# Cross-attention and MoE kernel: maxima over partitions by matrix transposes, an earlier load of x for group 1, a new order of small steps in the first group

## The reference

```python
# x, ctx: (4, 1024, 1024) f32; 4096 tokens in all, D = 1024
def fp8_quant_dequant(v):
    scale = 448.0 / max(max(abs(v)), 1e-12)          # one scale for the whole tensor
    return float8_e4m3(clip(v * scale, -448, 448)) / scale

x = x + fp8_qd(layernorm(x)) @ fp8_qd(ctx) + mask    # mask is a bias per batch and column
h = layernorm(x)
x = x + shared_ffn(h) + moe(h)
# shared_ffn: silu(h @ gate) * (h @ up) @ down, inner width 1024
# moe: 32 experts of inner width 512; sigmoid scores plus bias, best 3 of 8 groups, best 4 experts,
#      each expert takes its first 160 tokens (position = running count), silu(G) * U @ W_down, weighted add
```

## Time and profile before

| | us |
|---|---|
| median of 3 runs | 2037.12 (2036.63 to 2037.95) |
| the profiled execution | 2037.94 |
| its span | 2036.3 |
| TensorE busy | 1870.2 (92%) |
| VectorE busy | 1395.4 (69%) |
| ScalarE busy | 896.9 (44%) |
| GpSimd busy | 587.8 (29%) |
| mean granted TensorE clock | 0.991 of full |

### The profile page before, as it was taken

One profiled execution on the slowest core, in us unless ns is written; L12 is line 12 of the kernel. 1 busy time (PEld: TensorE's weight loads), 2 busy tenths in 40 slices (PEclk: granted clock), 3 DMA queues, 4 the chain that ended last, 5 costly groups with the idle time before them and its releaser, 6 DMA issues.

```text
span 2036.3 us, 45113 instructions
## 1 busy us (share of the span) xinstructions
PE 1870.2 (92%) x17857; PEld 1439.3 (71%) x17872; DVE 1395.4 (69%) x2535; ACT 896.9 (44%) x1269; POOL 587.8 (29%) x613
## 2 busy tenths in 40 slices
PE   0038999999999999999999999989999999999997
PEld 0017577678668668767767867858888888888886
DVE  5787775575575576566546535368888888888884
ACT  8564222222222222222212121157777777777774
POOL 2100101210220220220211111136555565655642
PEclk9998999999999999999999999999999999999999
DMA  9925322222222212312211211379999999999993
GB/s 378 373 70 197 95 82 73 84 63 64 84 62 75 93 44 74 94 62 62 76 63 43 63 63 53 135 259 357 371 353 363 368 347 374 349 367 363 355 369 86
DMA packets 93267, 371.94 MB, mean 183 GB/s; under 512 B 21264, under 2 KB 25392, under 8 KB 68560
## 3 DMA queue, kind: packets, MB, share of 16 engines
q1 hardware_dynamic: 68144, 311.16, 39.6%
q0 software_dynamic: 23808, 58.81, 13.2%
q10 hardware_dynamic: 1184, 0.15, 0.0%
HBM read 314.79 MB, written 55.35 MB: 182 GB/s over the span
## 4 chain that ended last, share of the span: by engine, by line
PE 88%; DVE 2%; DMA 1%; issue 1%; SPq 0%; POOL 0%; ACT 0%; POOLq 0%; ACTq 0%
PE ps L1277 52%; PE ps L1288 16%; PE ps L1456 8%; PE ps L1315 5%; PE ps L1464 2%; PE ps L1342 1%; PE ps L1418 1%; PE ps L1360 1%; DMA X<-in_x 1%; DMA BIG<-in_w_up 1%; PE ps L1298 1%; DVE W L966 1%; PE ps L1423 0%; PE ps L1366 0%; POOL out_rows L580 0%
## 5 line engine op out<-in xcount | busy, mean ns | idle before, releaser
L1277 PE MATMUL ps<-XT,W 128*128 128x256 f16 (+1 forms) x12288 | 1116.9, 253 | 7.9 <-DVE SG L1245 3.0
L1277 PEld LDWEIGHTS ps<-XT,W 128*128 128x128 f16 x12288 | 1025.6, 98 | 93.2 <-issue 14.8
L1220 DVE SCALAR_TENSOR_TENSOR W<-BIG,W 128x2048 f16<-128x2048 f32 x192 | 436.0, 2284 | 63.9 <-ACT W L802 63.7
L802 ACT ACTIVATE W<-BIG 128x2048 f16<-128x2048 f32 x192 | 361.4, 1900 | 8.5 <-DMA BIG<-in_w_gate 8.3
L1288 PE MATMUL ps<-W,HH 128*128 128x512 f16 x1536 | 339.2, 379 | 2.0 <-DVE e_pr L1093 2.0
L250 POOL TENSOR_TENSOR expo<-expo 128x1 f32<-128x1 f32 x159 | 83.1, 523 | 669.7 <-ACT FR L678 294.8
L1288 PEld LDWEIGHTS ps<-W,HH 128*128 128x128 f16 x1536 | 150.2, 98 | 176.6 <-DVE e_pr L1093 2.5
L744 ACT ACTIVATE SG<-ps 128x256 f32<-128x256 f32 x128 | 49.1, 384 | 469.5 <-PE ps L1277 469.5
L1139 DVE SCALAR_TENSOR_TENSOR SG<-ps,SG 128x256 f32<-128x256 f32 x128 | 54.3, 424 | 253.3 <-ACT SG L744 253.3
L513 POOL TENSOR_TENSOR rs<-ve,expo 128x1 f32<-128x1 f32 x32 | 17.9, 559 | 566.7 <-DVE ve L987 566.7
L570 POOL DMA_INDIRECT FR<-xn_rows,gix x64 | 165.6, 2587 | 31.6 <-issue 31.6
(11 more groups left out here) (172 smaller groups left out, 1773.2 us busy)
## 6 DMA issues: line engine op xcount, KB each, us to landing
BIG<-in_w_gate SPq DMA_DIRECT2D x64, 1024.0 KB, 8.8
BIG<-in_w_up SPq DMA_DIRECT2D x64, 1024.0 KB, 8.3
BIG<-in_w_down SPq DMA_DIRECT2D x64, 1024.0 KB, 8.2
X<-in_x SPq DMA_DIRECT2D x16, 1024.0 KB, 5.1
X<-in_mask POOLq DMA_DIRECT2D x16, 1024.0 KB, 8.3
xn_rows<-FR SPq DMA_DIRECT2D x32, 512.0 KB, 2.7
out_rows<-X SPq DMA_DIRECT2D x32, 512.0 KB, 2.7
W<-in_x SPq DMA_DIRECT2D x6, 2048.0 KB, 19.5
```

The costliest lines, as they stand in the source:

```text
L802: ac.activation(dst, stage, ACT.Copy, scale=W_SCALE).then_inc(x_hi, 1)
L1220: ve.scalar_tensor_tensor(out=lo[cut], in0=src, scalar=W_SCALE, in1=hi[cut], op0=ALU.mult, op1=ALU.subtract).then_inc(x_lo, 1)
L1277: ins = te.matmul(out_ps, a[:, k, cols], b[:, k, :], start=n == 0, stop=n == len(steps) - 1)
```

## The change

It does five things. The partition maxima are no longer taken by GpSimd: TensorE transposes the column of 128 values into one row in PSUM, VectorE takes the row's maximum and copies it 128 times into a row (`peak_spread_row`), TensorE transposes this back into a column, and `fp8_scale` reads that from PSUM; GpSimd keeps the root, now ahead of the maximum. The context's scale is made right behind that of x, ahead of the rounding of x, and "b" 3 is looked at ahead of both. The load of x for group 1 stands behind the last load of stage one, and the second lift buffer of ctx moves from X into W. The first split of VectorE stands behind the statistics of group 0. In group 0 VectorE reads the positions ahead of the additions for group 1, in all others where it did.

```diff
--- before.py
+++ after.py
@@ -162,7 +162,7 @@
         ctx_ring = [BIG[:, 16384 + 2048 * s:16384 + 2048 * (s + 1)].bitcast(F32) for s in range(2)]
         M_main = BIG[:, 22528:24576].bitcast(F32)
         lift_x = XT[:, :].bitcast(F32)
-        lift_ctx = [HH[:, :].bitcast(F32), X[:, 2048:4096]]
+        lift_ctx = [HH[:, :].bitcast(F32), W[:, 24576:28672].bitcast(F32)]
         ew_stage = [BIG[:, 4096 * m:4096 * (m + 1)].bitcast(F32) for m in range(6)]
         xbuf = [X[:, b * NT * D:(b + 1) * NT * D].rearrange("p (t d) -> p t d", t=NT) for b in range(2)]
         xn = [FR[:, j * D:(j + 1) * D] for j in range(NT)]
@@ -187,6 +187,9 @@
         dn_tail = PS[7][:, 0:TD]
         out_quarters = out.rearrange("t (c d) -> (t c) d", c=TQ)
         xn_quarters = xn_dram.rearrange("t (c d) -> (t c) d", c=TQ)
+        peak_row = lg[0:1, 0:P]
+        peak_in = [PS[n][0:1, 0:P] for n in range(2)]
+        peak_out = [PS[n][:, P:P + 1] for n in range(2)]
         logit_ps = PS[2][:, 0:G]
         score_ps = PS[3][:, 0:NT * E]
         pos_ps = PS[5][:, 0:NT * E].rearrange("p (t e) -> p t e", t=NT)
@@ -212,7 +215,8 @@
 
         x_sum, x_mean, x_square, x_norm, p1_done = map(sem, ("x_sum", "x_mean", "x_square", "x_norm", "p1_done"))
         a_lift = sem("a_lift")
-        amax_ready, amax_all, scales_ready = map(sem, ("amax_ready", "amax_all", "scales_ready"))
+        amax_ready, x_root, peak_across, peak_spread, peak_back, scales_ready = map(
+            sem, ("amax_ready", "x_root", "peak_across", "peak_spread", "peak_back", "scales_ready"))
 
         sw_hi, sw_lo, rw_hi, rw_lo = map(sem, ("sw_hi", "sw_lo", "rw_hi", "rw_lo"))
 
@@ -369,6 +373,7 @@
                 if piece == ("c", 5):
                     x_load(0, 0)
 
+            x_load(1, 1)
             sp.wait_ge(p1_done, max(p1_freed(piece) for piece in RING if p1_at(piece) > 3))
             for n in range(4):
                 sw_load(n)
@@ -384,9 +389,9 @@
 
             def group(g, r, front=True, ctx=2):
                 first = isinstance(g, int) and g == 0
-                if front:
-                    if first:
-                        sp.wait_ge(d_cq, 8)
+                if first:
+                    sp.wait_ge(d_cq, 8)
+                elif front:
                     wait(sp, st_out[1 - r], (g + r) * 16)
                     x_load(g + 1, 1 - r)
                 if first:
@@ -487,10 +492,7 @@
                 ch.sync()
             carry(gp, 2).then_inc(x_norm, 1)
             pool.wait_ge(amax_ready, 1)
-            ch.link(gp.partition_all_reduce(sc1[:, 1:2], sc1[:, 0:1], P, bass.bass_isa.ReduceOp.max))
-            gp.tensor_tensor(sc1[:, 1:2], sc1[:, 1:2], root[:, :], ALU.pow).then_inc(amax_all, 1)
-            pool.wait_ge(amax_ready, 2)
-            gp.partition_all_reduce(sc1[:, 5:6], sc1[:, 4:5], P, bass.bass_isa.ReduceOp.max).then_inc(amax_all, 1)
+            gp.tensor_tensor(sc1[:, 0:1], sc1[:, 0:1], root[:, :], ALU.pow).then_inc(x_root, 1)
             pool.wait_ge(x_norm, 1)
 
             def pool_carry(before):
@@ -885,11 +887,17 @@
                     dve.wait_ge(ld_p1[p1_at(piece)], 16 * p1_loads(piece))
                     abs_max(p1_slot[p1_at(piece)], c).then_inc(p1_done, 1)
 
+            def peak_spread_row(n):
+
+                dve.wait_ge(peak_across, n + 1)
+                ch.link(ve.tensor_reduce(sc1[0:1, 12 + n:13 + n], peak_in[n], AX.X, ALU.max))
+                ve.tensor_copy(peak_row, sc1[0:1, 12 + n:13 + n].to_broadcast([1, P])).then_inc(peak_spread, 1)
+
             def fp8_scale(n):
 
                 at = 4 * n
-                dve.wait_ge(amax_all, n + 1)
-                ch.link(ve.tensor_scalar(sc1[:, at + 1:at + 2], sc1[:, at + 1:at + 2], 1e-12, None, ALU.max))
+                dve.wait_ge(peak_back, n + 1)
+                ch.link(ve.tensor_scalar(sc1[:, at + 1:at + 2], peak_out[n], 1e-12, None, ALU.max))
                 ch.link(ve.reciprocal(sc1[:, at + 3:at + 4], sc1[:, at + 1:at + 2]))
                 ch.link(ve.tensor_scalar(sc1[:, at + 2:at + 3], sc1[:, at + 3:at + 4], FP8_MAX, None, ALU.mult))
                 ch.link(ve.reciprocal(sc1[:, at + 3:at + 4], sc1[:, at + 2:at + 3]))
@@ -932,13 +940,16 @@
                     ch.link(ve.tensor_tensor(xpeak[:, :], xpeak[:, :], xvar[:, :], ALU.mult))
                     ve.tensor_reduce(sc1[:, 0:1], xpeak[:, :], AX.X, ALU.max).then_inc(amax_ready, 1)
                 if piece == ("b", 2):
+                    peak_spread_row(0)
+                if piece == ("b", 3):
+                    ch.sync()
+                    ve.tensor_reduce(sc1[:, 4:5], amax[:, :], AX.X, ALU.max).then_inc(amax_ready, 1)
                     fp8_scale(0)
                     ch.do(ve.tensor_scalar(a1[:, :], a1[:, :], sc1[:, 2:3], None, ALU.mult))
                     ch.do(ve.tensor_scalar(b1[:, :], b1[:, :], sc1[:, 2:3], None, ALU.mult))
                     ch.sync()
                     ve.tensor_copy(sc1[:, 8:9], sc1[:, 2:3]).then_inc(scales_ready, 1)
-            ch.sync()
-            ve.tensor_reduce(sc1[:, 4:5], amax[:, :], AX.X, ALU.max).then_inc(amax_ready, 1)
+            peak_spread_row(1)
 
             def x0_round(j):
                 dve.wait_ge(a_lift, j + 1)
@@ -951,9 +962,9 @@
                     fp8_round_lifted(ctx0[m][:, cols], lift_ctx[m % 2][:, cols],
                                      BIG[:, (2 * m + t) * D:(2 * m + t + tiles) * D]).then_inc(d_cq, tiles)
 
-            x0_round(0)
             fp8_scale(1)
             ve.tensor_tensor(sc1[:, 9:10], sc1[:, 3:4], sc1[:, 7:8], ALU.mult).then_inc(scales_ready, 1)
+            x0_round(0)
             x0_round(1)
             for m in range(4):
                 ctx0_round(m, tiles=1 if m == 3 else 2)
@@ -1004,13 +1015,13 @@
                                             in1=xT[0][:, 4 * h:4 * h + 4, j * P:(j + 1) * P],
                                             op0=ALU.mult, op1=ALU.subtract).then_inc(d_xl, 1)
 
-            split_lo(0)
             add_cross(0, 0, 0)
             ln2_stats(0, 0, 0)
             add_cross(0, 0, 1)
             shift(0, 0)
             ln2_stats(0, 0, 1)
             shift(0, 1)
+            split_lo(0)
             split_lo(1)
             xt_lo(0, 0)
             xt_lo(0, 1)
@@ -1087,11 +1098,12 @@
                 ch.link(ve.tensor_tensor(r_w[:, :, :], r_w[:, :, :], r_den[:, :].unsqueeze(2).to_broadcast([P, NT, TOPK]),
                                          ALU.mult))
 
-            def route_slots(g):
-
+            def read_positions(g):
                 dve.wait_ge(pe_pos, g + 1)
                 ve.tensor_tensor(e_pr[:, :, :, :], e_eq[:, :, :, :],
                                  pos_ps.unsqueeze(2).to_broadcast([P, NT, TOPK, E]), ALU.mult).then_inc(d_pos, 1)
+
+            def route_slots(g):
                 dve.wait_ge(d_pos, g + 1)
                 ch.link(ve.tensor_reduce(r_pos[:, :, :], e_pr[:, :, :, :], AX.X, ALU.add))
                 ch.do(ve.tensor_scalar(r_ge[:, :, :], r_pos[:, :, :], float(C), NO_SLOT, ALU.is_ge, ALU.mult))
@@ -1156,9 +1168,12 @@
 
                         ctx_round(g, 2 * g + 9, 1, 2 * g + 10)
                     if ic == 4 and not front:
+                        read_positions(g)
                         route_slots(g)
                     dve.wait_ge(a_hh, n + 1)
                     ve.tensor_tensor(hT[1][:, ic, :], h32[ic % 2], hT[0][:, ic, :], ALU.subtract).then_inc(d_hl, 1)
+                if first:
+                    read_positions(0)
                 if front:
                     residual(g + 1, 1 - r)
                     for j in range(NT):
@@ -1166,6 +1181,8 @@
                 if first:
                     for n in FIRST_SPLITS[KS]:
                         split_lo(n)
+                if front and not first:
+                    read_positions(g)
                 if front:
                     route_slots(g)
                 if weights:
@@ -1397,6 +1414,11 @@
                          last_chunk=(d_hl, 8 * g + 8) if u == 0 else None).then_inc(pe_dn, 1)
 
             pe.wait_ge(consts_ready, 2)
+            for n, ready in ((0, x_root), (1, amax_ready)):
+                pe.wait_ge(ready, n + 1)
+                te.transpose(peak_in[n], sc1[:, 4 * n:4 * n + 1], identf[:, :]).then_inc(peak_across, 1)
+                pe.wait_ge(peak_spread, n + 1)
+                te.transpose(peak_out[n], peak_row, identf[0:1, 0:1]).then_inc(peak_back, 1)
             xq_transpose(0)
             cross_first()
             xt_transpose(0, 0)
```

## The result

The changed kernel takes 2026.60 us (median of 5 runs, 2025.34 to 2027.11), the kernel before 2037.12 (median of 5, 2035.22 to 2039.21): ratio 0.9946, 95% interval 0.9931 to 0.9961, so 8 to 14 us less. The forecast was 2027.2. The medians are 10.5 us apart. The profiled execution is the fastest of the five, 2025.34, with a span of 2023.7, 12.6 less than before.

A forecast was written before the change was run, and what follows sets the result against it. TensorE was taken as the bound, 88% of the span, with gains only at its waits before 246 us. 6.9 + 1.75 - 0.7 + 1.63 + 0.32 = 9.9 us gave 2027.2 us, range 2024.6 to 2031.2.

The forecast's parts named there:

- Stage one, scale of x: Ahead of group 0: transposes over TensorE replace GpSimd's reduction and its wait, so ScalarE starts at 99.95; gain 6.9 us.
- Scale of the context: Stage one: made ahead of x's rounding under ScalarE's lift, it leaves the path and a VectorE wait goes; gain 1.7 us.
- Order behind the rounds: Before group 0's first product: VectorE, its first split moved, waits for the unfinished cross product; cost 0.7 us.
- x of group 1: In group 0: with the earlier load, ScalarE waits only for stores and TensorE no longer waits; gain 1.63 us.
- Positions: Group 0, second down product: early read gains 0.3 us, not 2.04, since the product also waits for the last splits.
- A: Stage one: the transposes are no faster than the reduction, only 1.3 us gained, 2035.8 us; chance 0.03.
- B: Part of stage one is eaten by slow trips, uncovered splits or late loads; gain 6 to 8, 2030.3 us; chance 0.15.
- C: TensorE's clock does not fall near 204 us, after the 4.46 us wait; 1.5 us more, 2025.7 us; chance 0.17.
- D: TensorE's clock stays low longer in group 0, making the kernel slower, 2042 us; chance 0.04.
- The sum: Whole kernel: the terms add to a gain of 9.9 us, forecast 2027.2 us.

The follow-up runs named there:

- root_ahead: Changed kernel with the maxima back on GpSimd's reductions, in the new order, and the root ahead of both reductions; 2033.05 us.
- reduce_root_scalar: As scale_early, with GpSimd's two reductions in place of the four transposes and the root on ScalarE; 2023.98 us, ratio 0.9920 to the kernel before.
- split_first: Changed kernel with VectorE's first split back ahead of the additions of the cross product; 2027.02 us.
- x_late: Changed kernel with the load of x for group 1 at its old place in SP's queue; 2032.03 us.
- pos_late: Changed kernel with the read of group 0's positions back behind the last splits; 2027.74 us.
- scale_early: Changed kernel, first split at its old place, group 0's first normalised-row transposes before the second down product, x's scale before the last context peak; 2026.90 us.
- after_again: Changed kernel run once more with no edit, as the mark for its block; 2028.41 us, ratio 0.9941.
- best_xq_late: Changed kernel, first split at its old place; in group 0, first normalised-row transposes before the second down product, rounded x transposed behind the eighth product; 2027.67 us.

## Why the prediction was right

**Stage one, scale of x: right in size, wrong in its owner.** 6.9 was forecast and came (7.1 counted from the look at x's peaks). The pieces: transposes 0.37 and 0.26 for my 0.42, maximum and copy 0.27 and 0.21 for 0.19 each. What I called GpSimd's reduction was not one. I had noted that its printed 0.38 us were "no price: the root behind it waits 10.89 us", and put the wait on the reduction. The reduction is done in 0.4; the wait belongs to the root behind it, another kind of work (root_ahead, reduce_root_scalar, and the MODIFY_POOL_CONFIG pairs). The sum could not tell the two apart, as both go with the change, so that its size was right says nothing for its mechanism. The remedy could tell them apart: the transposes are the slower way over the partitions, by 1.83 us at the first rounding.

**Scale of the context: right.** 1.7 forecast, 8.7 in sum at the first context round. The second trip had its cover in ScalarE's lift, of which 1.71 us are left idle.

**Order behind the rounds: right, a loss.** 0.7 forecast, 0.65 by split_first.

**x of group 1: the mechanism right, the price a lower end.** The next thing late was the store, as said, and the product no longer waits. "Gain 1.63" was the wait of one execution; in x_late it was 2.43 and drew 1.67 of lower clock behind it. In the first pair of traces the stretch from the second product to the end of the wait for the rounded x is 1.8 us shorter, near the forecast; in the block of x_late the load is worth 3.8 to 5.0 by the medians, the lower end with the read of the positions in it. The step that failed is to take the length of a wait as its price when the clock hangs on it.

**Positions: right.** 0.3 forecast, 0.25 by pos_late, though the row named a wait of 2.04.

**The rivals.** A fell: VectorE's waits in all four trips are 0.35 us together. The rule of the Trainium skill cited with it ("VectorE: DVE Perf Modes", "Rules for kernel authors") is for the one step itself right after all: GpSimd's reduction is quicker. From the end of the context's maximum to the scale's first step it takes 0.49 us in reduce_root_scalar, the trip over TensorE 1.35 in scale_early. What the change got rid of is its neighbour. B fell: the first product stood 0.15 ahead of its forecast. C was half right: the clock fell behind the wait of 4.46 in every trace that has the wait, so it did not stay up, but by the moment of its rise the two products vary by 1.6 us each. That variation makes up nearly all of the 1.1 to 2.3 us by which the first trace ran ahead. D did not occur: the first product was never over 8.31, and the second took 5.41 or 5.42 in every trace.

**The sum.** By the first trace 12.2 at the second down product, less 2.16 of clock, is 10.1 against 9.9 forecast. The medians gave 10.5, and 12.2 when the pair ran again (after_again). That the first came within 0.6 us of the forecast is in part luck, since an early or late rise of the clock alone moves each of two products by up to 1.6 us.

## What to carry to other kernels

When an engine's row is short and the next one on it waits for "issue", ask which of the two instructions the time belongs to. Look at the source lines for instructions of the engine's queue that no timeline shows, and put each piece of work alone: here keeping the reduction and moving the root to another engine took 2.9 us more off the median than replacing the reduction did (2023.98 against 2026.90). A wait of TensorE has a price beyond its length if the clock falls behind it, so a cover for it can be worth more than the row says. Where the profile names one releaser, read the code for the other conditions of the same wait before counting the whole of it as a gain.

## What the runs showed of the hardware that I had not expected

GpSimd's `partition_all_reduce` of one value per partition takes 0.35 to 0.42 us in seven rows (an eighth, the second of the kernel before, is printed with 1.00). Going from element-wise work to it left GpSimd idle for 6.0, 6.1 and 9.6 us, and going back for 6.8, 7.1, 7.6, 10.05, 10.8 and 10.9, whether the element-wise operation was the root or an addition. The changes of 9.6 and more all began before 100 us, while the core's DMA engines were busy throughout (a share of 1.04 or more from 96 to 104 us in the kernel before); the shorter ones began at 104.2 or later, and from 106 to 112 us the share is 0. Whether transfers lengthen the change no run here shows. The change begins before the instruction's own wait: in reduce_root_scalar GpSimd ends its statistics at 85 us, the pair stands there, and the reduction that was released at 93.6 started at once.

The clock of TensorE fell behind a wait of 2.43 us in x_late (0.69 granted over the next 4 us, 1.67 us lost in three products), and behind one of 2.64 us in best_xq_late (0.50), while waits of 1.63 before and 1.79 to 2.04 ahead of the second down product did not lower it.

In the kernel before the granted clock reads 1.00 where the matmuls do not bear it out. A window and two rows of TensorE's timeline:

```profile
124.00:128.00 4.00, 3.57 (x8) 1.02 (x8) 3.86 (x4) 3.68 (x2) 0.00 (x0) 1.00 0.84 165
```

```profile
124.40 3.57 PE L1327 MATMUL ps<-BIG,FR 128*128 128x512 bf16 x8 [5.89 <-DVE BIG L909]
...
214.22 6.85 PE L1315 MATMUL ps<-BIG,FR 128*128 128x512 bf16 x31
```

Eight matmuls of 512 columns in 3.57 us are 446 ns each, 31 of the same size later 221 ns each: the first ones ran at 1.2 GHz, the lower level. In pos_late too the record reads 1.00 until 136 us, while 12 such matmuls from 127.44 on take 442 ns each. So the 1.00 that a trace here starts with says nothing of the level; behind its first change the record fits the rows in the changed kernel (0.50 from 124 to 132 us, and 12 matmuls from 127.69 on at 432 ns each).
